# One weight split per half of the heads instead of two, its copies moved from GpSimd to ScalarE and its transfers from GpSimd's queue to SyncE's, with new due times in the planner

## The reference, cut to what matters

```python
def reference(x, ctx, Wt, Wp, Wg, Wz, gn_w, gn_b, up, down, perm):   # x, ctx: (8, 512, 2048)
    x = x + xattn(layernorm(x), ctx, ctx, Wt, Wp, Wg, Wz, gn_w, gn_b)
    return x + ffn(layernorm(x), up, down, perm)

def xattn(q, k, v, ...):
    t = einsum('oc,bcd->bod', Wt, v); p = einsum('oc,bcd->bod', Wp, q); g = einsum('oc,bcd->bod', Wg, k)
    att = sum(p * g) over each of 8 channel groups        # one number for batch and group
    y = einsum('goi,bgid->bgod', Wz by group, att * t)
    return groupnorm(y) * gn_w + gn_b + v

def ffn(x, up, down, perm):                               # 16 heads of 128 columns, 512 hidden
    t = x[:, perm].reshape(rows, 16, 128)
    t = gelu(einsum('bhd,hdm->bhm', t, up))
    t = einsum('bhm,hmd->bhd', t, down)
    return t.reshape(rows, 2048)[:, inverse of perm]
```

## Time and profile before

| | us |
|---|---|
| three runs | 1638.12, 1641.98, 1646.77 |
| median | 1641.98 |
| profiled execution, its time | 1638.12 |
| its span, first to last instruction | 1636.3 |
| PE busy in it | 1534.8 |
| DVE, ACT, POOL busy | 1224.5, 975.8, 859.0 |
| granted TensorE clock, mean | 0.985 |

### The profile page before, as it was taken

How to read it: one execution, slowest core, us unless ns; L and a number is a source line. 1 busy time by engine, 2 the same in 40 slices (tenths; PEclk the granted TensorE clock), 3 DMA queues, 4 the chain that set the end, 5 groups by cost and what they waited for, 6 DMA issues and landing times.

```text
span 1636.3 us, 19309 instructions
## 1 busy us (share of the span) xinstructions
PE 1534.8 (94%) x6592; PEld 1240.4 (76%) x6592; DVE 1224.5 (75%) x1736; ACT 975.8 (60%) x1061; POOL 859.0 (52%) x781
## 2 busy tenths in 40 slices
PE   8899998998899999899999999999999999888997
PEld 6677876776678777688777887777877788666886
DVE  4788978796776977669786786867778687866665
ACT  4226466634686256672577636775367844795885
POOL 1380255176851667512585126841278223878885
PEclk9999999999999999999999999999999999999999
DMA  8878868887876856858366673858548485468685
GB/s 312 323 249 308 216 204 294 261 272 240 277 275 179 266 180 232 335 176 264 128 242 257 218 232 106 311 194 242 176 159 327 134 260 162 153 144 286 214 259 197
DMA packets 119985, 378.98 MB, mean 232 GB/s; under 512 B 24656, under 2 KB 24656, under 8 KB 111696
## 3 DMA queue, kind: packets, MB, share of 16 engines
q1 hardware_dynamic: 84304, 251.88, 45.8%
q0 software_dynamic: 35584, 125.86, 23.2%
HBM read 291.65 MB, written 86.03 MB: 231 GB/s over the span
## 4 chain that ended last, share of the span: by engine, by line
PE 58%; DVE 13%; DMA 9%; ACT 8%; issue 7%; POOL 4%; SPq 1%; POOLq 0%; ACTq 0%; DVEq 0%
PE PP L833 15%; PE PP L872 13%; PE PP L887 12%; PE PP L819 12%; PE PP L846 5%; DMA WW<-w_scratch 3%; ACT R L964 2%; DVE Z L1118 2%; DVE R L1001 2%; ACT R L906 2%; DVE X L1013 2%; DMA RAW<-in_cx 2%; DMA xg_scratch<-FB 1%; DVE HX L1153 1%; ACT PP L965 1%
## 5 line engine op out<-in xcount | busy, mean ns | idle before, releaser
L872 PE MATMUL PP<-GG,WW 128*128 128x512 f32 x1536 | 399.6, 397 | 26.1 <-DVE GG L1148 12.3
L819 PE MATMUL PP<-R 128*128 128x512 f32 x1536 | 357.6, 392 | 16.9 <-DVE R L1001 15.8
L833 PE MATMUL PP<-R,WC 128*128 128x512 f32 x1536 | 355.9, 393 | 10.1 <-DVE R L1007 7.5
L872 PEld LDWEIGHTS PP<-GG,WW 128*128 128x128 f32 x1536 | 292.1, 192 | 96.2 <-issue 23.2
L819 PEld LDWEIGHTS PP<-R 128*128 128x128 f32 x1536 | 288.3, 189 | 81.5 <-ACT R L906 11.3
L833 PEld LDWEIGHTS PP<-R,WC 128*128 128x128 f32 x1536 | 291.1, 190 | 73.9 <-issue 9.1
L887 PE MATMUL PP<-R,WW 128*128 128x512 f32 x1050 | 272.2, 395 | 12.0 <-DVE R L1153 9.6
L964 ACT ACTIVATE R<-PP 128x1024 fp32r<-128x1024 f32 x175 | 179.8, 1027 | 149.0 <-PE PP L872 145.6
L965 ACT ACTIVATE PP<-PP 128x1024 f32<-128x1024 f32 x256 | 261.5, 1022 | 0.0
L1238 POOL TENSOR_TENSOR FB<-FB,SMM 128x512 f32<-128x512 f32 x128 | 192.9, 1507 | 105.2 <-DVE GG L1148 79.7
L887 PEld LDWEIGHTS PP<-R,WW 128*128 128x128 f32 x1050 | 195.8, 189 | 61.0 <-issue 17.0
(11 more groups left out here) (92 smaller groups left out, 1631.9 us busy)
## 6 DMA issues: line engine op xcount, KB each, us to landing
WW<-w_scratch SPq DMA_DIRECT2D x160, 512.0 KB
RAW<-in_xT SPq DMA_DIRECT2D x64, 512.0 KB
RAW<-in_cT SPq DMA_DIRECT2D x64, 512.0 KB
X<-in_x SPq DMA_DIRECT2D x32, 1024.0 KB
RAW<-in_cx SPq DMA_DIRECT2D x32, 1024.0 KB
xg_scratch<-FB POOLq DMA_DIRECT2D x104, 256.0 KB, 4.9
w_scratch<-WW POOLq DMA_DIRECT2D x16, 1024.0 KB, 5.5
RAW<-in_Wg SPq DMA_DIRECT2D x8, 1024.0 KB
```

Of the source, the lines that this page charges most:

```text
L819: t = eng.matmul(s_bank(c1), l[:, part(c1)], r, start=(dt == 0 and j == 0), stop=(dt == ND - 1 and j == 2))
L833: t = eng.matmul(PP[2 + ot // 2][:, ot % 2, :], WC[:, l, ct, part(ot)], u[:, r + ct, :], start=(ct == 0 and j == 0), stop=(ct == NT - 1 an ...
L872: t = eng.matmul(PP[slot["up", f, p]][:, e, :], wt[:, l, part(2 * p + e)], g[:, r, :], start=(j == 0), stop=(j == 2))
```

## The change

It does five things. (1) `units(i)`: behind each batch from 2 on stand eight heads of two batches, heads 0 to 7 behind even batches and 8 to 15 behind odd ones; the number of steps of each stage stays. `load_w` falls from 160 transfers to 144. (2) Heads 0 to 7 are all split in the Y stage of batch 2, heads 8 to 15 still in the time of batch 0 but with other due times. Heads 0 and 1 stay in WW for the steps behind batch 2. (3) `w_hi` moves from POOL to ACT; `load_raw` and `keep_w` move from POOL's queue to SP's; `w_lo` stays on POOL. (4) The first three `load_s` of a batch are due 7.5, 6 and 4.5 units before s0 instead of 13, 10 and 7. (5) The `x1_piece`s stand about one unit earlier in DVE's order, in batch 7 two units apart instead of 1.33, and batch 7's layernorm and turns come later; `s_fix`, `s_evh` and `s_evl` get new due times.

```diff
-S_LOAD = (-13, -10, -7, -2.8, -1, 3.2, 4.8, 6.8)
+S_LOAD = (-7.5, -6, -4.5, -2.8, -1, 3.2, 4.8, 6.8)
...
     if i == 0:
         return []
+    half = [8 * (i % 2) + h for h in range(8)]
     if i == 1:
-        return [(h, [0]) for h in range(8, 16)]
-    if i == 2:
-        return [(h, [1]) for h in range(8, 16)] + [(h, [0, 1]) for h in range(4)]
-    if i == 3:
-        return [(h, [0, 1]) for h in range(4, 8)] + [(h, [2]) for h in range(8)]
-    half = [8 * ((i + 1) % 2) + h for h in range(8)]
+        return [(h, [0]) for h in half]
     ws = [(h, [i - 2, i - 1]) for h in half]
...
-        k = slot["wg", i] = slot["c", i, 3] if i in (2, 3) else ring("raw", NRAW)
+        k = slot["wg", i] = slot["c", i, 3] if i == 2 else ring("raw", NRAW)
...
-        return [("raw", slot["c", 2 + h // 4, 2 - h // 2 % 2])]
+        return [("raw", slot["c", 2, 2 - h // 2 % 2])]
...
     for k, h in enumerate((10, 11, 12, 13, 14, 15, 8, 9)):
-        t = 11 + 2.6 * k
+        t = 13.5 + 2.3 * k
         put(t, load_raw, h)
-        put(t + 4, w_hi, h)
-        put(t + 4.1, w_lo, h)
-        put(t + 4.2, keep_w, h)
+        put(t + 3.3, w_hi, h)
+        put(t + 3.5, w_lo, h)
+        put(t + 4.9, keep_w, h)
+    for k, h in enumerate((2, 4, 6, 0)):
+        t = 104 + (2.5, 5.2, 8.9, 12.1)[k]
+        for e in range(2):
+            put(t, load_raw, h + e)
+            put(109.6 + 3.3 * k + 1.6 * e, w_hi, h + e)
+            put(109.8 + 3.3 * k + 1.6 * e, w_lo, h + e)
+            put(111.1 + 3.3 * k + 1.6 * e, keep_w, h + e)
...
-        for k, h in enumerate(((), (), (2, 3, 0, 1), (6, 7, 4, 5))[i] if i < 4 else ()):
-            put(y0 + (2.5, 5.2)[k // 2], load_raw, h)
-            put(y0 + 5.6 + 1.8 * k, w_hi, h)
-            put(y0 + 5.7 + 1.8 * k, w_lo, h)
-            put(y0 + 5.8 + 1.8 * k, keep_w, h)
...
-            put(y0 + 11.3 + 0.6 * c1, s_fix, i, c1)
-            put(y0 + 11.5 + 0.6 * c1, s_evh, i, c1)
-            put(y0 + 12.2 + 0.6 * c1, s_evl, i, c1)
+            put(y0 + 11.9 + 0.7 * c1, s_fix, i, c1)
+            put(y0 + 12.1 + 0.7 * c1, s_evh, i, c1)
+            put(y0 + 12.5 + 0.7 * c1, s_evl, i, c1)
...
-            t = f0 + 5 + 0.8 * k if first else f0 + 7.95 + (1 if i == 1 else 1.33 if last else 2) * k
+            t = f0 + 5 + 0.8 * k if first else f0 + 6.97 + (2 * (k // 2) + 0.02 * hf if i == 1 else 2 * k)
...
-        e = f0 + 12 if first else f0 + 18.8 if last else base[i + 1] + 5.4
+        e = f0 + 12 if first else f0 + 22.4 if last else base[i + 1] + 5.4
...
-            t = base[i + 1] + TURN[i][q] if not last else e + 4.9 + 1.5 * q
+            t = base[i + 1] + TURN[i][q] if not last else e + 5.2 + 2 * q
...
-                if x < 2 and i in (1, 3):
+                if x < 2 and i < 3:
                     kept.append((w + x, j, h))
                     continue
                 t = w_used[w + x - 2][j]
-                t = max(t, v0 if i == 2 else y0 + 7 + 2 * x) if x < 2 else t
+                t = max(t, y0 + 7 + 2 * x) if x < 2 else t
...
+            elif stage == "w_hi":                       # in scalar(), in place of gpsimd()
+                h = a[0]
+                act.wait_ge(*at["rw", h])
+                for t in free["wsp", h]:
+                    act.wait_ge(*t)
+                eng.copy(WW[h % 2][:, 0:4:2, :], raw_tile(h)).then_inc(S["whi"], 1)
...
+            elif stage == "keep_w":                     # in sync(), as load_raw, in place of gpsimd()
+                h = a[0]
+                sp.wait_ge(*at["whi", h])
+                sp.wait_ge(*at["wlo", h])
+                eng.dma_start(w_d[h], f32(WW[h % 2][:])).then_inc(S[f"wk{h % 2}"], 16)
```

More of the change, by code:

```diff
@@ L39, in units @@
         return []
+    half = [8 * (i % 2) + h for h in range(8)]
     if i == 1:
-        return [(h, [0]) for h in range(8, 16)]
-    if i == 2:
-        return [(h, [1]) for h in range(8, 16)] + [(h, [0, 1]) for h in range(4)]
-    if i == 3:
-        return [(h, [0, 1]) for h in range(4, 8)] + [(h, [2]) for h in range(8)]
-    half = [8 * ((i + 1) % 2) + h for h in range(8)]
+        return [(h, [0]) for h in half]
     ws = [(h, [i - 2, i - 1]) for h in half]
     if i == B - 1:
-        rest = [8 + h for h in range(8)]
-        ws += [(h, [i - 1]) for h in rest[:4]] + [(h, [i - 1, i]) for h in rest[4:]]
-        ws += [(h, [i]) for h in range(ND) if h not in rest[4:]]
+        rest = [h for h in range(ND) if h not in half[4:]]
+        other = [8 * ((i + 1) % 2) + h for h in range(8)]
+        ws += [(h, [i - 1]) for h in other[:4]] + [(h, [i - 1, i]) for h in other[4:]]
+        ws += [(h, [i]) for h in range(ND) if h not in other[4:]]
     return ws
@@ L585, in plan @@
             put(t, load_c, i, q)
-        put(y0 + (9 if i in (2, 3) else 2.5 + late), load_wg, i)
+        put(y0 + (9 if i == 2 else 2.5 + late), load_wg, i)
         for q, t in enumerate((y0 - 3, y0 + 0.4, y0 + 4.3, y0 + 8.3)):
@@ L636, in plan @@
         put(e + 1.2, store_sd, i)
-        put(f0 + 30 if last else f0 + 29.5 if i == 0 else base[3] + 48.0 if i == 2 else e + 5, spread_sd, i)
+        put(f0 + 33 if last else f0 + 29.5 if i == 0 else e + 5, spread_sd, i)
         for ct in range(NT):
@@ L1167, in gpsimd @@
                 eng.tensor_tensor(GG[:], RAW[slot["wp"]][:], f32(HX[:]), ALU.subtract).then_inc(S["wpl"], 1)
[L1168 to L1179, removed]
-                eng.tensor_copy(WW[h % 2][:, 0:4:2, :], raw_tile(h)).then_inc(S["whi"], 1)
             elif stage == "w_lo":
@@ L1186, in gpsimd @@
                                   ALU.subtract).then_inc(S["wlo"], 1)
-            elif stage == "keep_w":
-                h = a[0]
-                pool.wait_ge(*at["wlo", h])
-                eng.dma_start(w_d[h], f32(WW[h % 2][:])).then_inc(S[f"wk{h % 2}"], 16)
             elif stage == "root_x":
@@ L1270, in sync @@
                 eng.dma_start(wp_d[:, 4:8, :], f32(GG[:])).then_inc(S["wpk"], 16)
+            elif stage == "load_raw":
+                h = a[0]
+                k = h % 2
+                for t in free["rw", h]:
+                    sp.wait_ge(*t)
+                eng.dma_start(raw_tile(h)[:, 0, :], up[h]).then_inc(S[slot["rw", h][1]], 16)
+                eng.dma_start(raw_tile(h)[:, 1, :].rearrange("p (t d) -> p t d", t=NM),
+                              down[h].rearrange("(t p) d -> p t d", p=P)).then_inc(S[slot["rw", h][1]], 16)
+            elif stage == "keep_w":
+                h = a[0]
+                sp.wait_ge(*at["whi", h])
+                sp.wait_ge(*at["wlo", h])
+                eng.dma_start(w_d[h], f32(WW[h % 2][:])).then_inc(S[f"wk{h % 2}"], 16)
             elif stage == "load_s":
```

## The result

The changed kernel takes 1651.87 us (median of 7 runs, 1646.34 to 1656.53), the kernel before 1641.98 beside it. The ratio is 1.0066, 95% interval 1.0039 to 1.0094: 0.7% slower, where 2.2% faster was forecast. The direction is wrong, and the time lies outside the range. Single executions of one kernel differ: the seven of the kernel before lie between 1633.51 and 1646.77 us. So the spans of the two profiled ones are 16.9 us apart (1653.2 and 1636.3), where the ratio stands for 10.8.

A forecast was written before the change was run, and what follows sets the result against it. PE bounds the kernel, busy 1534.8 of 1636.3 us, so its waits counted. Terms -19.3 - 5.8 + 4 - 10 + 0 - 2 - 3 = -36.1 gave 1602.0, or 1606 against 1642 as median; range 1588 to 1627.

The forecast's parts named there:

- the x1 pieces, -10: FFN, batches 2 to 6: x1_piece leaves the way of the first h_lo, 10 us less, bounds 6 and 12.
- Batch 3, -19.3: Batch 3: splits nothing and loads like batch 4, so its window falls from 212.0 to 192.7, 19.3 us less.
- The last rival: Batch 3's waits come from the bus, not the number of heads; its 19.3 shrinks to some 5: 1620 us, chance 0.05.
- Batch 2, Y and V, +4: Batch 2's Y stage and V: 10 us added by four more heads through two buffers, 6.3 removed; 4 us more.
- its FFN: Batch 2's FFN: weight buffers asked for every four units, so weight waits and slow clock go; 5.8 us less.
- Batch 0, -2: Batch 0: context loads go first, Y's first wait goes, a late w_hi gives that back; 2 us less.
- Batches 1 and 7, 0 and -3: Batch 1: no change, bounds 4 either way. Batch 7: x1_piece two units apart and turns save, gather costs; 3 us less.
- Keeps did not land fast: Rival: keep_w lands in 4.2 to 5.5 us, batch 2's Y and V lose nothing: 1596 us, chance 0.12.
- ACT behind `w_hi`: Rival: w_hi waits in ACT's queue for keep_w landings in batches 2 and 0: 1624 us, chance 0.12.
- The late S loads: Rival: first S loads of batches 2 to 7 land late: 1627 us, or 1650 if much later; chance 0.08.
- The side of slower: Whole kernel: the chance given to a result slower than the kernel before, 0.06.
- a granted clock under 1.00 in batches 4 to 6: Batches 4 to 6: a sign, named beforehand, that would show the forecast wrong.

The follow-up runs named there:

- late x1 pieces: The changed kernel with the x1_piece due half a gap after the second h_lo of their FFN step: 1639.72 us, ratio 0.9998.
- the later repairs: Reorderings of queues and due times in batches 2 and 0, added to the changed kernel with x1_piece behind the second h_lo and old s_fix times: 1627.06 to 1630.04 us.

## Why the prediction was wrong

**The failed step: the x1 pieces, -10.** It took a piece of 1.28 us at the new place too, counted the time that the pieces free ahead of the first `h_lo` and looked only at DVE's own queue at the new place. The same prediction had the rule and the row for what happens when a two-input operation of DVE meets one of POOL, and used them for `w_lo` alone; that `resid` is such an operation and runs just there was not asked. At the new place a piece lasts 2089 ns on the mean. Undoing the edit gives 12 us, so the term is about +12 in place of -10, the whole difference between no change and a loss. It isn't the whole miss: with the term at -10 the time would have been some 22 us less, about 1630, still outside the range. Placed behind the second `h_lo`, away from the first collision, the term was at most half its size (5 us in the kernel before, nothing in the changed one), and the 5 were not in the batches where it had been priced.

**A step that was missing: s_fix, s_evh, s_evl.** The prediction names their due times for batch 0 alone and gives 0 to the others. They cost 8 us, in waits of V.

**Batch 3, -19.3: right.** 18.0 with the x1 pieces undone, and PE has no wait for w_scratch there. The last rival (the change doesn't do what it says) falls. Whether the gain is from the splitting that went or from the fewer loads, no run takes apart.

**Batch 2, Y and V, +4: right mechanism, wrong size.** V starts 110.7 us behind S where it was 95.3, so 15.4 later. The waits of the old V stage that went (3.24 and 1.3 of slow clock) take off 4.5, the slow clock of the new one adds 2.4: some +13, an estimate from these rows, beyond the bound of 11; the four heads alone make 11.4. The sum took a landing of 7.5 us for the keeps where up to 11.3 were measured, and it had the rounds of the keeps only. That `load_wpl` stands behind the raw loads was seen, but not priced: it is issued 24 us later in the trace. Of V's wait only the last 3 us are its own, as the last `s_evl`, behind the `w_hi`s, ends at 386.7. The rest of batch 2, its FFN, became some 3.5 us shorter, where 5.8 and 1.2 for x1 were forecast.

**Batch 0, -2, measured +0.1.** Y starts at 57.9 in place of 63.3, as forecast, and gives it back, as forecast too: SP and PE of the changed kernel.

```profile
90.83 0.34 SPq L1320 DMA_DIRECT2D vs_scratch<-scol  x1
...
92.54 1.82 SPq L1272 DMA_DIRECT2D w_scratch<-WW  x1
```

```profile
84.70 12.54 PE L833 MATMUL PP<-R,WC 128*128 128x512 f32 x48 [4.41 <-DVE R L1013]
101.73 4.64 PE L833 MATMUL PP<-R,WC 128*128 128x512 f32 x13 [4.50 <-ACT Z L924]
```

The `w_lo` of head 12 ended at 81.79, and its keep is issued at 92.54, behind `store_sum`.

**Batches 1 and 7, 0 and -3.** Batch 1 lost 5.1, past its bound of 4; with late x1 pieces and the old s_fix times it takes 147.8 us, 1.3 less than before. Batch 7 took 362.3 us and not 358.0; with the same two repairs it takes 357.8, so the 3 us forecast for it were not seen.

**Added up.** The forecast missed by some 47 us (-36 and +11). From these runs, as an estimate: 22 are the x1 pieces, 8 the s_fix times, 9 batch 2's Y and V, and the other terms 1 to 3 each.

**The rivals.** Keeps did not land fast (8.1 in the median). ACT behind `w_hi` did become a gate in batch 2, but beside the DMA engines, not alone. The late S loads, the one rival on the slow side, were not the cause. The side of slower had been given one mechanism and 0.06, and what made the kernel slower was none of those priced. One of the signs of being wrong, a granted clock under 1.00 in batches 4 to 6, could tell nothing: batch 6 had 0.99 already.

**What stays open.** Why the new x1 times cost 3 us in the kernel before and 12 in the changed one; the stages of batches 2 and 3 make the difference, and no run takes them apart. What batch 2 would cost with less traffic at equal work was not tried: splitting two or four of its heads in batch 1 is the obvious next step, since with late x1 pieces and the old s_fix times every order tried inside batch 2 gave 1626 to 1630 us. These kernels are 0.6 to 1.3% faster than the kernel before; the later repairs add nothing that can be told.

## What to carry to other kernels

When an instruction is moved in one engine's order, lay the other engine that shares its SBUF ports beside the new place, and check every two-input operation there, not only those that the change touches. When a stage's DMA engines are near full, take landings from such a stretch (the keeps took 8.1 us in the median, 5.5 before), ask when each queue gets round to issuing what PE waits for, and look for the wait that ends next: here, to put the waiting item first moved the wait and gained nothing that could be measured. A due time that looks like a small shift can turn two overlapping chains into one that alternates: write down the order per engine and not the times.

## What the hardware showed that was not expected

The operation whose record starts first is not always the one that runs first. At 1058.35 of the changed kernel the piece starts 0.38 us ahead of `resid`'s operation, and it is the piece that waits; at 1028.37 of the kernel before the piece starts ahead of one as well and keeps its 1.28, while `resid`'s, from 1028.91, takes 1.90. And the hold-up goes both ways in turn, so one piece among two operations of POOL costs both engines: 2.76 in place of 1.28, and 2.16 in place of 1.30.
